# One-hots of the segment-sum units in wide vector operations, all dst comparisons on VectorE, sorted places copied from PSUM in pairs

## What is computed

```
h   = relu(layernorm(x))
m   = relu(relu([h[dst], edge_attr] @ W1.T + b1) @ W2.T + b2)      # per edge, 128 features
agg = segment_sum(m, src) / max(count(src), 1)                     # per node
z   = relu([h, agg, u[0]] @ Wa.T + ba)
out = x + z @ Wb.T + bb
```

## Time and profile before

| | us |
|---|---|
| median of 3 runs | 1935.99 |
| lowest and highest run | 1925.9, 1936.51 |
| span of the profiled execution | 1917.2 |
| first scatter of GpSimd starts, last one starts | 69.1, 1853.9 |
| TensorE busy | 1737.8 |
| VectorE busy | 1289.0 |
| ScalarE busy | 1433.6 |
| GpSimd busy | 1528.8 |

### The profile page before, as it was taken

One profiled execution on the slowest core, in us unless ns is written; L12 is line 12 of the kernel. 1 busy time (PEld: TensorE's weight loads), 2 busy tenths in 40 slices (PEclk: granted clock), 3 DMA queues, 4 the chain that ended last, 5 costly groups with the idle time before them and its releaser, 6 DMA issues.

```text
span 1917.2 us, 43265 instructions
## 1 busy us (share of the span) xinstructions
PE 1737.8 (91%) x12472; PEld 1470.5 (77%) x12472; DVE 1289.0 (67%) x4235; ACT 1433.6 (75%) x2975; POOL 1528.8 (80%) x991
## 2 busy tenths in 40 slices
PE   6898888999999999999999999999999999978837
PEld 4677666888888888888788788888888888867725
DVE  8565555667767676777776777777776676756727
ACT  4788887878888877788788787878877877862306
POOL 8488888888888888888888888888888888888850
PEclk8999999999999999999999999999999999998969
DMA  9988888999999999999999999999999999999856
GB/s 329 269 166 151 151 151 149 187 198 193 198 192 192 201 190 196 201 192 192 200 197 187 185 199 198 200 193 197 204 194 198 191 199 199 197 183 234 176 116 217
DMA packets 319400, 372.10 MB, mean 194 GB/s; under 512 B 42272, under 2 KB 203264, under 8 KB 318528
## 3 DMA queue, kind: packets, MB, share of 16 engines
q1 hardware_dynamic: 182400, 305.12, 55.6%
q0 software_dynamic: 135360, 62.15, 34.4%
q10 hardware_dynamic: 1408, 2.03, 0.3%
HBM read 203.87 MB, written 159.27 MB: 189 GB/s over the span
## 4 chain that ended last, share of the span: by engine, by line
POOL 44%; issue 19%; PE 17%; DMA 11%; DVE 5%; ACT 3%; SPq 1%; ACTq 0%; POOLq 0%; DVEq 0%
POOL sums L821 39%; DMA sums<-regA,idx 7%; POOL sums L809 5%; PE bank L1361 4%; PE bank L1350 4%; PE bank L1399 3%; PE bank L1373 3%; DVE regC L1215 2%; PE bank L1389 1%; DMA regC<-slots 1%; DMA regA<-sums 1%; DMA sums<-vscat,vidx 1%; ACT regA L931 1%; DVE regC L1182 1%; PE bank L1275 1%
## 5 line engine op out<-in xcount | busy, mean ns | idle before, releaser
L821 POOL DMA_INDIRECT sums<-regA,idx x844 | 1333.9, 1580 | 291.7 <-issue 244.4
L1350 PEld LDWEIGHTS bank<-h,regC 128*128 128x128 f32 x3072 | 389.0, 194 | 183.1 <-ACT h L943 134.0
L1350 PE MATMUL bank<-h,regC 128*128 128x130 f32 x3072 | 421.7, 281 | 63.0 <-ACT h L943 62.8
L1373 PE MATMUL bank<-regA,L 128*128 128x512 f32 x806 | 435.8, 623 | 4.6 <-DVE regA L1147 3.0
L1399 PE MATMUL bank<-w,h 128*128 128x128 f32 x3224 | 431.3, 277 | 0.0
L923 ACT ACTIVATE h<-bank,b1c 128x512 f32<-128x512 f32 x403 | 275.7, 684 | 198.0 <-PE bank L1373 193.1
L1399 PEld LDWEIGHTS bank<-w,h 128*128 128x128 f32 x3224 | 398.0, 194 | 1.1 <-ACT h L923 0.6
L1215 DVE TENSOR_SCALAR regC<-lows,regC 128x128 f32<-128x128 f32 x1176 | 257.7, 315 | 147.6 <-DMA regC<-slots 124.0
L1361 PE MATMUL bank<-regC 128*128 128x129 f32 x2352 | 298.3, 281 | 34.4 <-issue 19.0
L943 ACT ACTIVATE h<-bank 128x512 f32<-128x512 f32 x403 | 240.9, 598 | 111.1 <-PE bank L1399 107.2
L1361 PEld LDWEIGHTS bank<-regC 128*128 128x128 f32 x2352 | 277.2, 193 | 41.8 <-issue 38.1
(11 more groups left out here) (142 smaller groups left out, 1540.3 us busy)
## 6 DMA issues: line engine op xcount, KB each, us to landing
regC<-slots SPq DMA_DIRECT2D x294, 260.0 KB, 5.6
regA<-in_ea SPq DMA_DIRECT2D x202, 256.0 KB
slots<-regC SPq DMA_DIRECT2D x192, 260.0 KB
src<-rows_src SPq DMA_DIRECT2D x107, 256.0 KB
slots<-regC SPq DMA_DIRECT2D x192, 138.1 KB
sums<-regA,idx POOLq DMA_INDIRECT x844
dstR<-rows_dst SPq DMA_DIRECT2D x101, 128.0 KB
sums<-zeros SPq DMA_DIRECT2D x20, 645.0 KB, 7.0
```

What stands on the lines that cost most here:

```text
L821: nc.gpsimd.indirect_dma_start(out=sums[k], out_offset=bass.IndirectOffsetOnAxis(ap=idx[:, n % RING, t:t + 1], axis=0), in_=scat[:, n % 4, ...
L1350: last = T.matmul(psSlot(t)[:, k, :], place, h2[:, g % 2, t, :], start=True, stop=True)
L1373: T.matmul(psL1(s % 2), L[:, s % RING, :], R[:, s % RING, :], start=True, stop=True).then_inc(l1_done, 1)
```

## The change

Three edits in one:

1. The one-hots of a unit: instead of eight tensor_scalar of 128x128, two scalar_tensor_tensor of 128x512, one per bin for all four tiles. The key of a row is no longer a per-partition scalar but the first tensor operand, broadcast along the 128 columns; `lows` is the second, broadcast over the tiles. Both lie in SBUF.
2. The dst one-hot of every group is made by VectorE (line 1147 of before). The two ScalarE operations, the column `oh_bias` and the semaphores `oh_act_ready`, `oh_far` and `oh_bias_ready` go.
3. The places are copied out of PSUM two tiles at a time: one ScalarE operation of 520 columns per partition for tiles 0 and 1, and one for 2 and 3. It waits for both tiles; tile 2 waits for the first copy, tile 3 for nothing new. `slot_ready` counts two per group instead of four, and its waits elsewhere are rewritten to match.

```diff
@@ SP, before a row of dst is loaded
-                        wait(sp, oh_ready, sum(1 for g in range(GPP * (i - 1)) if not is_sorted(g)))
-                        wait(sp, oh_act_ready, sum(1 for g in range(GPP * (i - 1)) if is_sorted(g)))
+                        wait(sp, oh_ready, GPP * (i - 1))
@@ ScalarE
-            def evac_slots(g, t):
-
-                n = BINNED_NO[g]
-                act.wait_ge(slot_done, TPG * n + t + 1)
-                if t == 0:
+            def evac_slots(g, pair):
+
+                n, t = BINNED_NO[g], 2 * pair
+                act.wait_ge(slot_done, TPG * n + t + 2)
+                if pair == 0:
                     wait(act, slot_out[n % 2], 32 * (n // 2))
                     wait(act, vpre_ready, n - 1)
-                nc.scalar.activation(slot_sb[:, n % 2, :, t, :], psSlot(t), ACT.Copy).then_inc(slot_ready, 1)
+                nc.scalar.activation(slot_sb[:, n % 2, :, t:t + 2, :].rearrange("p h t c -> p t h c"), psSlots, ACT.Copy).then_inc(slot_ready, 1)
...
                 if is_sorted(g):
                     evac_slots(g, 0)
-                    evac_slots(g, 1)
...
                 if is_sorted(s - 2):
-                    evac_slots(s - 2, 2)
-                    evac_slots(s - 2, 3)
-                g = s + 2
-                if is_sorted(g):
...
-                    nc.scalar.activation(R[D:P, g % RING, :], dB[D:P, i % 2, g % GPP, :], ACT.Abs, bias=oh_bias[D:P, :]).then_inc(oh_far, 1)
+                    evac_slots(s - 2, 1)
                 if 1 <= s and s + 1 < NG:
                     seed(s + 1)
-                if is_sorted(g):
-                    act.wait_ge(oh_far, n + 1)
-                    nc.scalar.activation(R[D:P, g % RING, :], R[D:P, g % RING, :], ACT.Relu, bias=1.0, scale=-1.0).then_inc(oh_act_ready, 1)
@@ VectorE
                 g = s + 1
-                if 0 <= g < NG and not is_sorted(g):
+                if 0 <= g < NG:
...
                     for i in range(nb):
-                        for t in range(TPG):
-                            made = VE.tensor_scalar(oh2[0:rows, m % 2, i, t, :], lows[0:rows, i, :], loaded(m)[0:rows, i, t, C:W], -float(b), ALU.subtract, ALU.is_equal)
+                        made = VE.scalar_tensor_tensor(out=oh2[0:rows, m % 2, i, :, :], in0=loaded(m)[0:rows, i, :, C:W].broadcast_to([rows, TPG, LO]), scalar=float(b),
+                                                       in1=lows[0:rows, i, :].unsqueeze(1).broadcast_to([rows, TPG, LO]), op0=ALU.subtract, op1=ALU.is_equal)
                     made.then_inc(oh2_ready, 1)
@@ TensorE
-                if t >= 2:
-                    pe.wait_ge(slot_ready, TPG * n + t - 1)
+                if t == 2:
+                    pe.wait_ge(slot_ready, 2 * n + 1)
...
-                    pe.wait_ge(oh_ready, sum(1 for g in range(s + 1) if not is_sorted(g)))
-                    wait(pe, oh_act_ready, sum(1 for g in range(s + 1) if is_sorted(g)))
+                    pe.wait_ge(oh_ready, s + 1)
```

More of the change, by code:

```diff
@@ L342, in build @@
         oh_row = sb("oh_row", [P, 1], f32)
-        oh_bias = sb("oh_bias", [P, 1], f32)
         scrapc = sb("scrapc", [P, 1], f32)
@@ L385, in psSlot @@
             return bank[:, 6 + t % 2, 0:2 * W].rearrange("p (h c) -> p h c", h=2)
+        psSlots = bank[:, 6:8, 0:2 * W].rearrange("p t (h c) -> p t h c", h=2)
         def psZ(c):
@@ L604, in _ @@
                     n = BINNED_NO[s - QLAG]
-                    sp.wait_ge(slot_ready, TPG * (n + 1))
+                    sp.wait_ge(slot_ready, 2 * (n + 1))
                     sp.dma_start(slots[n, 0:HEAD, :], slot_sb[OVER:P, n % 2, 0, :, :].rearrange("p t c -> p (t c)")).then_inc(slot_out[n % 2], 16)
@@ L776, in scatter_all @@
                 n = BINNED_NO[g]
-                pool.wait_ge(slot_ready, TPG * (n + 1))
+                pool.wait_ge(slot_ready, 2 * (n + 1))
                 if g - 1 >= 0:
@@ L1110, in _ @@
             link(VE.scalar_tensor_tensor(out=oh_row[:, :], in0=viol[:, 2:3], scalar=-1e6, in1=winrow[:, :], op0=ALU.mult, op1=ALU.add))
-            VE.tensor_scalar(oh_bias[:, :], oh_row[:, :], -1.0, None, ALU.mult).then_inc(oh_bias_ready, 1)
             dve.wait_ge(srcF_ready, 1)
@@ L1200, in _ @@
                     n = BINNED_NO[s - VPRE]
-                    dve.wait_ge(slot_ready, TPG * (n + 1))
+                    dve.wait_ge(slot_ready, 2 * (n + 1))
                     if n >= 2:
@@ L1324, in free_sums @@
                 elif is_sorted(g):
-                    pe.wait_ge(slot_ready, TPG * (BINNED_NO[g] + 1))
+                    pe.wait_ge(slot_ready, 2 * (BINNED_NO[g] + 1))
             def free_row(s):
@@ L1454, in _ @@
             pe.wait_ge(scat_ready, len(PLAIN))
-            pe.wait_ge(slot_ready, TPG * NH)
+            pe.wait_ge(slot_ready, 2 * NH)
             pe.wait_ge(vscat_ready, NV)
```

3 lines of the change are left out of this document (removed).

## The result

| | before | after |
|---|---|---|
| median of 20 runs each, taken side by side | 1927.95 us | 1936.06 us |
| lowest and highest | 1921.3, 1938.03 | 1930.56, 1946.54 |
| span of the profiled execution | 1917.2 | 1935.0 |

The ratio after / before is 1.0042, with a 95% interval of 1.0027 to 1.0056. The changed kernel is slower by 8 us, 0.4%. The forecast was +21 us on a median of three runs, 1935.99, that stands 8 us above the median of 20. For the changed kernel each run's span is listed beside its time: the profiled run took 1936.77 us with a span of 1935.0, so 1.8 us lie around it, not 18.8. With the same 1.8 us, the profiled execution of before was one of some 1919 us, shorter than any of the 20.

A forecast was written before the change was run, and what follows sets the result against it. GpSimd's scatters were taken as the bound. One-hots +17 and dst comparisons +5 made +22, less 3 of waits plus 2 for price: +21, span 1917.2 to 1938, median 1935.99 to 1957 us; own range 1947 to 1968.

The forecast's parts named there:

- The bound: GpSimd issues 940 scatters nearly without pause: 1739 us of the span, with only 47 us of longer scatters and waits.
- The signs that were named: Scatters: median stays 1.545 us, mean about 1.605, long ones start inside new one-hots; few index waits; ScalarE some 1135 us busy.
- Unit one-hots: On VectorE, 294 new operations hold scatters for 20.4 us, less 3.2 for the old ones: +17 us.
- w x w / 3.8: Average hold per VectorE operation: w is its duration less 0.18 us; scatters start every 1.90 us.
- Dst comparisons: 192 more of line 1147 on VectorE hold scatters: +5 us, bounds 0 and +44.
- Places in pairs: ScalarE's 768 copies become 384 larger ones, covered in front of GpSimd: 0 us.
- Start and end: Ahead of the first scatter ScalarE loses 1.3 us and VectorE gains 0.5: 0, within a microsecond.
- the last term of the sum: GpSimd's landing waits shrink by perhaps 3 of 13 us; a possibly low hold price gives 2 back: +22 becomes +21.
- at 18.8 us around the span: Time outside the profiled span, added to the forecast span of 1938 us to give a median of 1957.
- N: Rival: the new one-hots on VectorE hold no scatter; +2 us, 1938; chance 0.15.
- S: Rival: both one-hot operations of a pair hold one scatter through; +51 us, 1987; chance 0.06.
- F: Rival: GpSimd is not the bound; relieving ScalarE shortens TensorE's waits; faster, 1911; chance 0.04.

The follow-up runs named there:

- e15: The changed kernel with half of the unit sums' matmuls left out: median 1935.7 us, 1.0038 against the kernel before.
- e1: The kernel before with only the new unit one-hots, two scalar_tensor_tensors of 128x512: median 1936.4 us, ratio 1.0040.
- e2: The kernel before with only the dst comparisons of all groups on VectorE: median 1930.6 us.
- e8: The changed kernel without its dst edit, so ScalarE keeps its dst comparisons: median 1935.7 us, 1.0039 to the kernel before.
- e3: The kernel before with only the places copied two tiles at a time: median 1933.5 us, 1.0045 to the kernel before.
- e16: The kernel before, unchanged, profiled again to catch an execution near the median: that execution took 1927.94 us.
- e9: The kernel before without the second of ScalarE's two operations on a sorted group's dst comparison: median 1925.6 us, ratio 1.0008.
- e5: The kernel before with the src comparison as four tensor_scalars of 128x128 in place of one tensor_tensor of 128x512: median 1927.3 us.
- e7: The changed kernel with both one-hot bins of a unit in one scalar_tensor_tensor of 128x1024, lows in half precision: median 1955.8 us.
- e13: The kernel before with half of the unit sums' matmuls left out: median 1924.8 us, 0.9968 to the kernel before.
- e17: The kernel before with VLAG 6 in place of 5, so GpSimd issues line 809's scatter one step later: median 1926.5 us.
- e6: The changed kernel with its unit one-hots as eight scalar_tensor_tensors of 128x128 in place of two: median 1931.5 us.

## Why the prediction was wrong, and where it was right

**The bound: right.** GpSimd's scatters set the changed kernel's time: median scatter 1546 ns, waits of 6 us in 940 scatters, and no gain from 84 us less of TensorE (e15). The signs that were named came out: the mean scatter is 1607 ns (1605 forecast), and the lengthened ones start inside the new one-hots. Off the path, VectorE is busy for 1355.4 us where 1324 were forecast.

**Unit one-hots: right.** Forecast were 20.4 us of holds. Summed over the scatters of the changed kernel's trace that start inside line 1197, the time above 1.545 us is 19.2 us (99 scatters; e1 19.4, e15 20.1). The rule "until the end, less 0.13 us" held to a hundredth of a microsecond in the rows shown, at 0.68 and at 1.22 us of length, and none of the 99 is held beyond the operation in which it starts; the longer one behaved as w x w / 3.8 asks (144 operations of 1.22 us: 144 x 1.04 x 1.04 / 3.8 = 41 us; 43 found). The lower bound, no hold, fell with it. The Trainium skill, SBUF — State Buffer, section "Who interferes with whom", says that tensor_tensor takes only the read interface of the shared ports, and infers from this why it was not seen to stall DMAs that GpSimd issues. This case's trace differs: a scalar_tensor_tensor with two SBUF inputs made the scatter at 362.59 0.51 us longer.

**Dst comparisons: right in size in the holds, not seen in the time.** +5 was forecast; scatters that start inside line 1130 have 8.7 us above 1.545 us in all, against 2.7 to 6.0 for line 1147 in the five profiles of before, so +3 to +6. e2 is at 1.0016, with an interval that holds both no change and +5 us; e8 shows no change.

**Places in pairs: right for the changed kernel, not by itself.** The cost was taken as 0 "as long as GpSimd does not wait". Alone (e3) the pairs cost 3.6 us by the medians, 8.7 by the ratio, by GpSimd's waits; with 54 or 57 us of holds beside them there is no such wait (e8, after).

**Start and end: right.** The first scatter starts at 69.4 us, against 69.1.

**The step that failed** is the last term of the sum: "longer scatters leave landings more time, which takes perhaps 3 of the 13 us of waits". It was mis-sized, since the 13 us came from one execution of 1919 us, and so did the premise that "the engines in front are ahead". An execution of before at the median has 22 us (e16), of which 12.7 end with ScalarE's copies and not with landings; the changed kernel has 6. So the term is -16, not -3: the landings gave the 3 that were forecast, and the waits for ScalarE's copies, which the sum put at nothing, gave 13. 25 us more holds (24 forecast) less 16 us of waits is 9, beside the +8 measured. It is the holds that take those waits, not the work that ScalarE was freed of: e8 keeps that work, and its waits for ScalarE's copies are gone too, while e9 drops half of it and keeps them; with the holds down to 17 (e5) such waits grow to 26 us above the usual gap. The -16 itself rests on one execution at the median of each kernel. Between the two executions that were profiled first, with waits of 13 and 6, the forecast would have done: spans of 1917.2 and 1935.0, +18 for +21.

**The second error** is the step "at 18.8 us around the span". Spans and times lie 1.8 us apart in every run listed. The 17 us that were too many were the sign that the profiled execution was not a median one, and the text took them for overhead instead. The forecast also stands on a median of three that is 8 us above the median of 20. Of the 21 us between 1957 and the measured 1936, these are 8, and the waits are the other 13.

**The rivals.** N fell (e1, e7). S fell in the changed kernel: a pair lets the scatter go after its first operation. F was wrong in its result, and the work taken from ScalarE is not what made the loss small (e8, e9). What it had right is that GpSimd by itself does not set the time of before. It was dismissed for "8 waits for indices in 940"; the waits that mattered end with `vscat` and `scat`, and that execution had none longer than the usual gap.

What stays open is which resource sets the pace in front of GpSimd at some 1925 us. It is not ScalarE's load alone (e9), not TensorE's alone (e13, which takes a third of a percent), and not the place of line 809 in the order alone (e17). That it is the loop through several engines together was not tried.

## What to carry to other kernels

When an engine is the bound by a narrow margin, a delay put on it costs only what exceeds the slack that it had already been losing to late inputs, and a delay taken from it gives back only until the inputs are late. So set the holds and the waits of that engine side by side, in more than one execution: span beside time tells whether the profiled one was a typical one. On VectorE, the length of single operations on SBUF operands, not their total, is what GpSimd's indirect DMAs felt here: the same one-hots cost 19 us of holds at 0.68 us each and 43 at 1.22.

## What the runs showed of the hardware that was not expected

In a row of eight short scalar_tensor_tensors without gaps (0.287 us each, e6), 24 of 142 scatters were held through one or two further operations, up to 0.43 us, most of them from the seventh operation to the end of the row. The tensor_scalars in the earlier trace rows held one by 0.07 us, and a pair of 0.68 us let every scatter go in between. Cutting an operation into pieces therefore took more away with tensor_scalar (e5: 17.0 us of holds in the src comparisons down to 0.8) than with this one (19.2 to 11.8).

How much the same 211 src comparisons hold depends on how they fall against the scatters: summed as above, 17.0 us in the first profile of before, 16.5 to 19.0 in the four others, 20.9 in the changed kernel, 12.7 in e1 and 29.0 in e2, with the same operation at 0.69 us. An estimate that takes the phases as even, 14.7 us here, can be off by a factor of two for one operation.
